# Two waits of GpSimd for TensorE's counts in every step of a graph attention kernel

## What is computed

```python
q = (x @ q_w.T + q_b).reshape(n, HEADS, HEAD_DIM)
k = (x @ k_w.T + k_b).reshape(n, HEADS, HEAD_DIM)
v = (x @ v_w.T + v_b).reshape(n, HEADS, HEAD_DIM)
row, col = (edge_index[0], edge_index[1])
scores = jnp.einsum('ehd,ehd->eh', q[row], k[col]) / jnp.sqrt(jnp.float32(HEAD_DIM))
scores = scores + edge_emb @ eb_w.T + eb_b
seg_max = jax.ops.segment_max(scores, row, num_segments=n)
exp_scores = jnp.exp(scores - seg_max[row])
seg_sum = jax.ops.segment_sum(exp_scores, row, num_segments=n)
attn = exp_scores / (seg_sum[row] + 1e-10)
out = jax.ops.segment_sum(attn[..., None] * v[col], row, num_segments=n)
return out.reshape(n, HIDDEN) @ out_w.T + out_b
...
x = _layernorm(x + _L0_gnn_ref(x, edge_index, edge_attr_128, ...), axis=-1)
```

## Time and profile before

| | |
|---|---|
| median of 3 executions | 3136.17 us (3133.39 to 3141.1) |
| the profiled execution | 3146.63 us |
| its span, first to last instruction | 3144.9 us |
| PE, PEld, DVE, ACT, POOL busy | 60, 48, 51, 50, 56% of the span |
| indirect transfers in ranking (L624) | 832, mean 983 ns, idle before them 612.3 us |
| indirect transfers in attention (L1087) | 880, mean 964 ns, idle before them 616.0 us |
| granted TensorE clock, mean | 0.717 of full speed |

### The profile page before, as it was taken

One profiled execution on the slowest core, in us unless ns is written; L12 is line 12 of the kernel. 1 busy time (PEld: TensorE's weight loads), 2 busy tenths in 40 slices (PEclk: granted clock), 3 DMA queues, 4 the chain that ended last, 5 costly groups with the idle time before them and its releaser, 6 DMA issues. The chain is left out here.

```text
span 3144.9 us, 58004 instructions
## 1 busy us (share of the span) xinstructions
PE 1899.1 (60%) x14721; PEld 1498.0 (48%) x14722; DVE 1604.0 (51%) x4853; ACT 1587.6 (50%) x3672; POOL 1758.0 (56%) x1783
## 2 busy tenths in 40 slices
PE   8755666655556666556265666666665565665654
PEld 8644444444444444444154454554544444554543
DVE  9433333333333333333155666666565666666675
ACT  9555555555555555555044454444454444454433
POOL 6355555555555555555645556556555555555515
PEclk9877777777777777777566666766676676667666
DMA  4222222222222222221123333333333333323323
GB/s 157 80 73 73 72 72 64 70 70 64 71 72 72 72 69 65 72 64 53 53 73 88 84 82 87 83 85 85 82 86 83 84 85 85 83 83 87 82 64 95
DMA packets 161607, 245.59 MB, mean 78 GB/s; under 512 B 44647, under 2 KB 105003, under 8 KB 161289
## 3 DMA queue, kind: packets, MB, share of 16 engines
q0 software_dynamic: 70528, 133.75, 15.9%
q1 hardware_dynamic: 83914, 107.72, 11.9%
q10 hardware_dynamic: 7111, 3.47, 0.4%
HBM read 216.09 MB, written 28.70 MB: 78 GB/s over the span
## 5 line engine op out<-in xcount | busy, mean ns | idle before, releaser
L1087 POOL DMA_INDIRECT attend_kv<-kv_rows,attend_rec x880 | 848.6, 964 | 616.0 <-issue 266.6
L624 POOL DMA_INDIRECT sorted_records<-rank_record,rank_row x832 | 817.5, 983 | 612.3 <-PE rank_slot_ps L706 350.7
L1151 PE MATMUL attend_sum_ps<-attend_wv,attend_hot 128*128 128x136 f32 x1760 | 364.4, 382 | 171.1 <-ACT attend_piece L1260 97.2
L1151 PEld LDWEIGHTS attend_sum_ps<-attend_wv,attend_hot 128*128 128x128 f32 x1760 | 333.3, 279 | 204.1 <-issue 201.3
L1116 PE MATMUL attend_q_ps<-q,attend_hot_t 128*128 x2640 | 312.3, 246 | 168.1 <-issue 162.9
L822 DVE TENSOR_TENSOR rank_before<-rank_same_ps,below 128x512 bf16<-128x512 f32 x208 | 139.4, 689 | 399.9 <-PE rank_same_ps L674 287.5
L1116 PEld LDWEIGHTS attend_q_ps<-q,attend_hot_t 128*128 128x128 bf16 x2640 | 222.0, 106 | 241.5 <-issue 201.6
L1219 ACT ACTIVATE attend_off<-attend_lo_ps,attend_neg_row 128x512 bf16<-128x512 f32 x220 | 150.2, 683 | 327.5 <-remote 272.0
L758 ACT ACTIVATE rank_off<-iota_r,neg_lo 128x128 bf16<-128x128 bf16 x800 | 245.3, 391 | 0.0
L1302 DVE TENSOR_TENSOR acc<-attend_sum_ps,acc 128x136 f32 x880 | 221.5, 296 | 43.2 <-remote 31.5
L840 DVE COPY rank_record<-meta 128x24 int32 (+1 forms) x104 | 18.5, 178 | 428.6 <-PE rank_slot_ps L706 399.3
(11 more groups left out here) (293 smaller groups left out, 4391.8 us busy)
## 6 DMA issues: line engine op xcount, KB each, us to landing
rank_edges<-in_edge_attr SPq DMA_DIRECT2D x103, 512.0 KB
rank_lo_rows<-lo_by_tile SPq DMA_DIRECT2D x104, 256.0 KB
attend_kv<-kv_rows,attend_rec POOLq DMA_INDIRECT x880
sorted_records<-rank_record,rank_row POOLq DMA_INDIRECT x832
sorted_records<-prepare_blank POOLq DMA_DIRECT2D x8, 888.0 KB, 12.0
attend_rec<-sorted_records SPq DMA_DIRECT2D x110, 64.0 KB
merge_rows<-prepare_zero POOLq DMA_DIRECT2D x2, 1800.0 KB, 24.0
kv_rows<-rank_kv_out SPq DMA_DIRECT2D x49, 64.0 KB
```

What stands on the lines that cost most here:

```text
L624: pool.indirect_dma_start(rec_dram[:, :], bass.IndirectOffsetOnAxis(ap=row[:, v, t:t + 1], axis=0), record[:, v, t, :], None).then_inc(sca ...
L1087: pool.indirect_dma_start(kv[:, v, t, :], None, kv_dram[:, :], bass.IndirectOffsetOnAxis(ap=rec[:, v, t, H + 2:H + 3], axis=0)).then_inc(k ...
L1151: mm = pe.matmul(sum_ps[:, bank, i * W:(i + 1) * W], hot[:, u, t, :], wv[:, v % 4, t, :], start=True, stop=True)
```

## The change

Ranking: the wait for `slots_ready` moves from the fifth transfer to the sixth (t = 5), and a new wait for `next_ready` of s + 3, which is TensorE's `count_up` in its step s + 2, stands before the second (t = 1). Attention: the wait for `turned` moves from the fifth transfer to the first (t = 0), beside that for `weighted`; a new wait for `keys_turned` of s, the end of TensorE's step s - 2, stands before the fifth. The first eight steps of attention, not four, go without them.

```diff
             for t in range(G):
-                if t == G // 2 and not until(k, v, 4) and inside(k, v, 2):
+                if t == 1 and not until(k, v, 4) and inside(k, v, 3):
+                    pool.wait_ge(next_ready, s + 3)
+                    pool.sem_inc(c["carrier"], 1)
+                if t == 5 and not until(k, v, 4) and inside(k, v, 2):
                     pool.wait_ge(slots_ready, s + 2)
                     pool.sem_inc(c["carrier"], 1)
...
             for t in range(G):
-                if t == G // 2 and not until(k, v, 4):
+                if t == 0 and not until(k, v, 8):
                     pool.wait_ge(turned, s - 1)
+                    pool.sem_inc(c["carrier"], 1)
+                if t == 4 and not until(k, v, 8):
+                    pool.wait_ge(keys_turned, s)
                     pool.sem_inc(c["carrier"], 1)
```

## The result

The kernel after takes 3167.44 us (median of 4 runs, 3162.1 to 3173.19), the kernel before 3138.64 us (4 runs, 3133.39 to 3144.94). The ratio is 1.0091, with a 95% interval of 1.0069 to 1.0113. The forecast was 3105 us, faster; the time is inside its range and on its other side. The profiled execution of after took 3162.1 us, 5.3 us less than its median, and that of before 3146.63 us, 8 us more than its own. So the two traces differ by 15.5 us where the medians differ by 28.8 us. What follows is the balance of the traces.

A forecast was written before the change was run, and what follows sets the result against it. No engine is full; a loop of waits between GpSimd and TensorE sets the pace. 3146.6 + 10 (ranking) - 41 (attention) = 3115.6 us, less the profiled execution's 10.5 above the median: 3105 us, range 3020 to 3245.

The forecast's parts named there:

- The loop of before: Both stages: GpSimd waits for TensorE, whose signals come late during GpSimd's transfer runs; 13.67 us a ranking step, 13.25 in attention.
- GpSimd's runs don't hold TensorE: Rival, both stages: signals are late for a reason of TensorE's own, so nothing moves; 3136 us, chance 0.15.
- the copy at 827.02: Ranking: ScalarE's copy starts 7.1 us after the bias matmuls it waits for, 1.8 us after GpSimd's run ends.
- L706 comes 5.0 us after `count_up`: Ranking, first step of a pair: `slots_ready` comes at 814.5 under a run of four, the time of before.
- the one run of four in the earlier trace: Ranking, 179.65 to 184.40: `slots_ready` 5.0 us after `count_up`, read as a run of four costing TensorE nearly nothing.
- the slower rival: GpSimd tied too closely, idle 2.4 to 3 us twice a step: 3242 or 3243 us (one stage, 0.21), 3380 (both, 0.14).
- held L706: Ranking, first step of a pair: `slots_ready` comes 2.3 us after the run, at 817.4, 2.9 us more; +147 us.
- The second step of the pair: Ranking: a run of 12, or one ending early; the pair changes by 0 to +0.4 or by -0.7 us.
- the bound +147: Ranking's slow bound: `slots_ready` held in the first step of each pair, 2.9 us in each of 50 pairs.
- The term was -41: Attention: runs of eight, never 12, a step of 12.85 instead of 13.25 us, for 102 steps -41 us.
- Attention's half of it: Attention in the slower case: `keys_turned` and `turned` each seen only after a run of four, 14.2 us a step, +97 us.

## Why the prediction was wrong

**The loop of before** was read rightly: on a chip where TensorE's and SyncE's signals aren't held, the idle time behind L706 is gone and a pair takes 20.48 instead of 27.30 us, with the same durations of transfers and matmuls. The rival "GpSimd's runs don't hold TensorE" is wrong for the traces that were forecast from, and right for the four chips of the experiments, where the change does nothing (1.0006). The Trainium skill's page "SBUF — State Buffer", section "SBUF: two separate sides", says of the engines' ports to SBUF that TensorE never waits on anyone and that only VectorE's and GpSimd's shared port pair causes contention. The four chips agree with it. In the first traces TensorE's signals are late beside GpSimd's runs, by the copy at 827.02 and the one at 789.82, but no run shows that a port is what they wait for; the forecast took the rule to cover more than it says.

**The step that failed** is "L706 comes 5.0 us after `count_up`", in ranking's first step of the pair. It came 6.9 us after, in the 36 passes of 44 in which the step was split (mean of the step 16.17 instead of 14.31 us). It was valued by the one run of four in the earlier trace rows, and that case was misread. There the run had begun 1.7 us before `count_up` ended, and so was over 3.1 us after it; L706, 5.0 us after `count_up`, stood 1.96 us after the run's end. That is near the 2.3 us that were read from the ends of longer runs. The bias matmuls were recorded until 185.44, 1.0 us after the run, so neither of the signals that are late elsewhere was due while the run lasted. The row could not tell "not held" from "held to the end of a run that ends early", and 5.0 us happened to be the undisturbed time too. In the changed kernel the run begins 0.8 us after `count_up` by construction, ends 5.6 us after it, and L709's signal comes 1.2 to 1.5 us behind that (in the 7 late steps 3.2, 7.9 and 1.0 to 1.2 us). The prediction's own rule for the slower rival, that it decides when a signal isn't out before the run is three or four us old, pointed the same way: 5.0 us after `count_up` is 4.2 us into the run. The "held L706" was on the list as a bound, at 2.9 us a pass with a lateness of 2.3 us; with the measured 1.3 us it is 1.9.

Two slips of the working change nothing here: 50 x 2.9 is 145 and not 147, and 0.40 less a tenth of it plus 0.10 is 0.46; the 0.48 takes off half of that tenth.

**The second step of the pair** was forecast with runs of twelve, or with one that ends early, for 0 to +0.4 or -0.7 us. Since L709 is seen only after the run of four, the next run is a whole one of eight. The step takes 12.71 instead of 12.99 us, -0.28. What was not foreseen is that the split step doesn't recur each time: in 8 of 44 pairs `count_up` was there already, by 3.4 us or more, and the step took 12.68 us, which took back 0.3 us a pair. Ranking in all: forecast +10, measured +40.9 us, the bound +147.

**Attention** went the way that was forecast. The runs of eight rose from 11 to 66 and the undisturbed step is 12.7 us (forecast 12.85 as a mean), but 12 twelves and 28 fours are left, where the forecast had none of twelve. The term was -41 and is -27.1 us; from the 11th step to the 101st a step takes 12.92 us where before has 13.27, and the stage's first and last steps give some of that back. That attention's gain comes from the hold is argued from the pattern of runs. Without a hold the two waits gave nothing (1.0004 twice) or cost 14 us, which fits, but no run took them apart on a chip that holds signals.

**The rivals.** The slower one, "a wait for a signal that is itself held by the run before it", is the mechanism that decided, in ranking only, and at 1.5 us a pair rather than 2.9. Attention's half of it didn't happen. The sum with the measured terms is 3146.6 + 40.9 - 27.1 = 3160.4, and with some 2 us at the seams the 3162.1 of the profiled execution.

**What stays open.** Why TensorE and SyncE are held during GpSimd's runs where before takes 3138 us, and not on the four chips where it takes 2454 to 2458 us. Nothing in the programs differs, and the recorded durations of their work do by a few per cent at most. Which of ranking's two waits costs on the first kind of chip was not tried there. Nor was the version with attention's new waits and ranking's old one; by the traces it would be 3138.6 - 27 = some 3112 us (an estimate from the two stages), and it would beat both kernels. On the other chips it is no better than before.

## What to carry to other kernels

A single row that agrees with "undisturbed" must be checked against the other reading: measure the signal's distance from the end of the run as well as from the work before it, and where both fit, give them equal weight. A wait that releases GpSimd on a signal in the middle of another engine's step starts a run on top of the rest of that step; where runs delay signals, as in the trace of after, the next signal costs the whole run, so the last signal of a step, not an early one, is the place to try first (ranking's old wait was of this kind and took 27.30 us a pair against 28.25; no other place was tried). And a wait for a newest count is free only as long as it never ends last: with no hold at all it cost 14 us in attention once TensorE was close.

## What the hardware showed that was not expected

The same program with the same durations of transfers (0.96 us and 0.30 between) and of matmuls took 3138 us where the first traces were taken and 2454 to 2458 us on the four chips of the experiments. What differs in the traces is when TensorE's signals come, and some of SyncE's own instructions, 74 of 763 of which take 0.59 to 0.94 us there, where none takes more than 0.08 us elsewhere.

Twice the sums in each of 110 steps cost 5 us in all (2460.28 against 2455.29 us). The granted clock rose from 0.74 to 0.90, so TensorE was busy only 0.9 us more a step, and it still ended within GpSimd's 10.11 us: work added to a TensorE that waits was nearly free.
